# Output stores issued by ScalarE, and attention slots one group later, in a linear-attention block on eight cores

## The reference

```python
xn = layernorm(x)                      # no weight or bias here
q, k, v = xn @ Wq + bq, xn @ Wk + bk, xn @ Wv + bv
qf, kf = elu(q) + 1, elu(k) + 1        # heads of 128, chunks of 128 tokens
kv_ex, ksum_ex = sums of kf^T v and of kf over the chunks before
out = (qf kv_ex + causal(qf kf^T) v) / (qf ksum_ex + rowsum(causal(qf kf^T)) + 1e-6)
s = out @ Wo + bo
Wt = clip(round(W / mean|W|), -1, 1)   # ternary weights
g = silu((xn * ln_w + ln_b) @ Wt)
y = x + s * g
```

## Time and profile before

| | us |
|---|---|
| median of 3 runs | 2493.84 (2489.82 to 2498.37) |
| the profiled execution | 2509.68 |
| its span on the slowest core (core 4) | 2508.1 |
| spans of cores 0 to 7 | 2477.6, 2494.0, 2464.4, 2476.5, 2508.1, 2486.8, 2467.7, 2455.6 |
| mean granted TensorE clock, cores 0 to 7 | 0.990, 0.986, 0.990, 0.988, 0.985, 0.988, 0.991, 0.990 |

### The profile page before, as it was taken

The page is one execution under the profiler, slowest core; times in us unless marked ns, Lnnn a source line. Parts: engine busy times, 40 slices in busy tenths (PEclk is TensorE's granted clock), DMA queues, the critical chain, the costliest instruction groups (busy, mean ns, idle before and its releaser), DMA issues.

```text
span 2508.1 us, 38029 instructions; the slowest of 8 cores (2455.6 to 2508.1 us)
## 1 busy us (share of the span) xinstructions
PE 2397.4 (96%) x12618; PEld 1144.3 (46%) x12618; DVE 1168.0 (47%) x2448; ACT 698.8 (28%) x1241; POOL 245.1 (10%) x452
## 2 busy tenths in 40 slices
PE   5998999999999999998999999999999999999998
PEld 3444444444444444543444444554444445554443
DVE  6134766555521454554552144555554135554443
ACT  4144545223300343421220133441221024442000
POOL 1100000011111000011120000001111100000110
PEclk9999999999999999999999999999999999999999
DMA  8997877897755655569985554557998555555652
GB/s 213 209 208 173 171 174 169 187 214 201 177 102 88 97 91 96 102 160 213 212 173 106 94 93 91 113 104 182 228 183 164 91 105 99 101 103 113 161 158 73
DMA packets 264477, 363.31 MB, mean 145 GB/s; under 512 B 184416, under 2 KB 184416, under 8 KB 256096
## 3 DMA queue, kind: packets, MB, share of 16 engines
q0 software_dynamic: 56320, 201.36, 40.6%
q1 hardware_dynamic: 188672, 125.87, 22.8%
q10 hardware_dynamic: 19296, 33.66, 5.4%
HBM read 411.14 MB, written 41.94 MB: 181 GB/s over the span
## 4 chain that ended last, share of the span: by engine, by line
PE 73%; DMA 20%; DVE 4%; issue 2%; SPq 1%; ACT 0%; DVEq 0%; ACTq 0%; POOL 0%; POOLq 0%
PE pj L949 40%; PE pj L963 28%; DMA ktok<-kh 7%; DMA y<-xy 6%; DMA xy<-x 4%; DMA wscf<-wpr 2%; DVE bst L682 1%; PE px L991 1%; PE pa L977 1%; DMA ring<-w_v 1%; PE po L1010 1%; PE po L1007 1%; DVE to L853 1%; DVE to L858 1%; SPq L367 0%
## 5 line engine op out<-in xcount | busy, mean ns | idle before, releaser
L949 PE MATMUL pj<-ring,big 128*128 128x512 bf16 x6144 | 1351.0, 382 | 36.7 <-DVE to L853 27.2
L949 PEld LDWEIGHTS pj<-ring,big 128*128 128x128 bf16 x6144 | 601.8, 98 | 768.6 <-issue 65.8
L963 PE MATMUL pj<-big,ring 128*128 128x512 bf16 x4096 | 935.8, 383 | 0.0
L963 PEld LDWEIGHTS pj<-big,ring 128*128 128x128 bf16 x4096 | 394.1, 99 | 439.4 <-issue 18.9
L714 DVE TENSOR_TENSOR big<-pj,brow 128x512 bf16<-128x512 f32 x128 | 88.4, 691 | 329.3 <-PE pj L949 329.3
L839 DVE SCALAR_TENSOR_TENSOR tf<-pj,r,c_b 128x512 f32<-128x512 f32 x128 | 94.9, 747 | 175.4 <-PE pj L949 140.5
L533 ACT ACTIVATE ee<-pj,bk 128x512 f32<-128x512 f32 x128 | 88.0, 688 | 261.6 <-PE pj L963 261.6
L533 ACT ACTIVATE ee<-pj,bq 128x512 f32<-128x512 f32 x128 | 88.1, 688 | 259.1 <-PE pj L963 256.3
L564 ACT ACTIVATE sg<-tf 128x512 bf16<-128x512 f32 x128 | 79.2, 630 | 290.1 <-DVE tf L839 262.9
L464 POOL DMA_DIRECT2D ring<-w_qk x128 | 67.8, 544 | 930.4 <-PE pj L963 560.3
L861 DVE TENSOR_TENSOR xy<-to,xy 128x512 f32<-128x512 f32 x128 | 88.6, 692 | 121.6 <-DMA xy<-x 102.6
(11 more groups left out here) (79 smaller groups left out, 1442.0 us busy)
## 6 DMA issues: line engine op xcount, KB each, us to landing
ring<-w_qk POOLq DMA_DIRECT2D x128, 512.0 KB, 10.8
ring<-w_v POOLq DMA_DIRECT2D x64, 512.0 KB, 12.5
stg<-w_f SPq DMA_DIRECT2D x32, 1024.0 KB, 8.3
ring<-wscf POOLq DMA_DIRECT2D x64, 512.0 KB, 7.6
ring<-w_o POOLq DMA_DIRECT2D x64, 512.0 KB, 10.1
xy<-x ACTq DMA_DIRECT2D x128, 256.0 KB, 5.2
y<-xy POOLq DMA_DIRECT2D x128, 256.0 KB, 7.6
xln<-x SPq DMA_DIRECT2D x28, 1024.0 KB, 8.7
```

Source lines behind the costliest of these rows:

```text
L949: last = tensor.matmul(bank[:, :], src(k, m), ring[c % 3][:, k * 512:(k + 1) * 512], start=(k == 0), stop=(k == NT - 1))
L963: last = tensor.matmul(bank[:, :], ring[c % 3][:, base + k * 256:base + k * 256 + 128], x[:, k * T + tok:k * T + tok + 512], start=(k == 0 ...
```

## The change

`store_y` moves from POOL's program to ScalarE's. ScalarE calls it at the start of a step, for the output step before, so it waits there for that product (s_yd); the final waits for all stores move with it. `slot_units` counts slots from t - 1, so every `outputs`, `scores` and `outer`, with what VectorE, ScalarE and SyncE do for them, falls one slot later; LAST_SLOT becomes 69. `transpose_k` keeps its slots, 4h+2 and 4h+3. `outputs`, `scores` and `transpose_out` are now in odd slots, `outer` in even ones.

```diff
--- before.py
+++ after.py
@@ -30,7 +30,7 @@
 QK0 = 32
 FO0 = 96
 NCHUNK = 20
-LAST_SLOT = 68
+LAST_SLOT = 69
 NB = 3
 
 
@@ -115,7 +115,7 @@
 
 def slot_units(t):
 
-    hh, r = divmod(t, 4)
+    hh, r = divmod(t - 1, 4)
 
     def head(h, s):
         return (h, s) if 0 <= h < H else None
@@ -465,15 +465,6 @@
                                      in_=src[:, j * D:(j + 1) * D]
                                      ).then_inc(s_w[sl][j], 16)
 
-            def store_y(k):
-                pn, m = divmod(k, 8)
-                p, n = divmod(pn, 4)
-                g = p * MT + m
-                gpsimd.wait_ge(s_yd, k + 1)
-                gpsimd.dma_start(
-                    out=y_out[g * 128:(g + 1) * 128, n * 512:(n + 1) * 512],
-                    in_=xy[k % 4][:, :]).then_inc(s_ys[k % 4], 16)
-
             load_chunk(0)
             gpsimd.wait_ge(s_xn, 5)
             load_chunk(1)
@@ -484,14 +475,6 @@
                     c = p * NCHUNK + (i + 1) // 8 + 2
                     if i % 8 == 7 and c < NP * NCHUNK:
                         load_chunk(c)
-                    k = p * NG + i - 1
-                    if k > FO0 and (k % NG == NG - 1 or i - 1 >= FO0):
-                        n, m, o = of_fo(k % NG)
-                        if o:
-                            store_y((k // NG * 4 + n) * 8 + m)
-            store_y(NP * 32 - 1)
-            for i in range(4):
-                gpsimd.wait_ge(s_ys[i], 16 * (NP * 32 // 4))
 
         @block.scalar
         def _(scalar):
@@ -608,6 +591,15 @@
                                in_=x_in[g * 128:(g + 1) * 128, n * 512:(n + 1) * 512]
                                ).then_inc(s_xr[k % 4], 16)
 
+            def store_y(k):
+                pn, m = divmod(k, 8)
+                p, n = divmod(pn, 4)
+                g = p * MT + m
+                scalar.wait_ge(s_yd, k + 1)
+                scalar.dma_start(
+                    out=y_out[g * 128:(g + 1) * 128, n * 512:(n + 1) * 512],
+                    in_=xy[k % 4][:, :]).then_inc(s_ys[k % 4], 16)
+
             def copy_x(m):
 
                 p = m // MT
@@ -640,6 +632,12 @@
             for p in range(NP):
                 for i in range(NG):
                     t = i - QK0
+
+                    k = p * NG + i - 1
+                    if k > FO0 and (k % NG == NG - 1 or i - 1 >= FO0):
+                        n, m, o = of_fo(k % NG)
+                        if o:
+                            store_y((k // NG * 4 + n) * 8 + m)
                     if QK0 <= i < FO0:
                         evict_qk(p, t)
                     if 0 <= t <= LAST_SLOT:
@@ -659,6 +657,9 @@
                             load_xr(p, n, m)
                         if o and 2 <= m < 6:
                             load_xr(p, n, m + 2)
+            store_y(NP * 32 - 1)
+            for i in range(4):
+                scalar.wait_ge(s_ys[i], 16 * (NP * 32 // 4))
 
         @block.vector
         def _(vector):
```

## The result

Beside the kernel before on the same chip, the changed kernel takes 0.9942 of its time, with a 95% interval of 0.9914 to 0.9971. Of the 2493.84 us this is some 14 us less (2493.84 × 0.9942 = 2479). The medians of 19 runs each, 2489.34 and 2497.42 us, lie a little nearer to each other because some runs of both were disturbed (a whole die at a lower clock); the ratio leaves those out. The profiled execution took 2468.98 us, some 10 us less than the ratio gives. The forecast was 2440 us with a range of 2415 to 2478 us: right in sign, four times too large in size, and the time is outside the range.

What follows compares the result with a forecast made beforehand. The prediction took TensorE's waits on the slowest core, some 110 us idle, as the bound. From the profiled execution, 2509.7 − 43 (attention shift) − 27 (y stores) = 2440 us, range 2415 to 2478 us.

Steps and rivals of the forecast that it cites:

- What bounds the kernel: Slowest core: the matmul engine is busy 96% of the span, so the gain lies in TensorE's waits, some 110 us idle.
- What the shift gives: TensorE's ktok waits: 3.0 us more slack each removes 33.3 us, and 10 us of clock come back; −43 us.
- Together 7.3 us: What remains of the five ktok waits on TensorE that exceed the 3.0 us of slack gained.
- What the shift costs in pass 0: VectorE's state update behind ternary work in odd slots: still 0.6 us early, 0 us; 12 us if that cover is gone.
- The sign named for it: In pass 0, TensorE waits at L1007 for L550 or L759 would show the forecast wrong.
- I take 5 us: Time of a y store on ScalarE's queue, by the xy loads of equal size there; bounds 2.3 and 16.4 us.
- Rival (a): Moving the y stores gives nothing, as the DMA engines are shared and 0.89 busy: 2467 us, chance 0.13.
- The new wait is hardly longer than the old one: ScalarE's wait for s_yd: the product of m−1 comes only 3.45 us after that of m−2, whose store loads await anyway.
- Rival (c): On ScalarE's queue each refill stands behind a store, both taking 14.6 us: slower, 2547 us, chance 0.07.
- The term of −27 us: Gain from y stores on ScalarE's queue: 17 us at L853, 3.2 at L839, 3.4 at L1056, 3.4 of slow groups.
- the forecast's own marks: Among them: VectorE's 102.6 us at L861 below 50; stores about 5 us; ktok waits under 12 us; none at L1007.
- The other waits at L853 go: TensorE's output-projection eviction waits of 3.1 us and less vanish; of 27.2 us there, 17 go.

Runs made afterwards that it cites:

- `x_on_tensor`: Attention shift, y stores on POOL, TensorE transposing the normalised x in all passes in place of DMA transposes, against the kernel before: 0.9868 [0.9842, 0.9894].
- `wait_only`: Attention shift, y stores on POOL, ScalarE still made to wait for each product (s_yd), against the kernel before: 0.9864 [0.9836, 0.9892].

## Why the prediction was wrong, point by point

**What bounds the kernel: right.** From run to run the mean span went with TensorE's idle time: 106.8 us idle and 2507.2 with the loads one step later, 68.3 and 2456.2 after, 61.7 and 2449.9 with the shift, 39.3 and 2421.7 with the shift and copies. Only where TensorE got more work, in `x_on_tensor`, did it not.

**What the shift gives: right in mechanism, too large in size.** "Together 7.3 us" of ktok waits should stay; 5.2 us stayed on the slowest core and 2.0 us on average. The term was −43 us; the shift alone gave −24 us by its ratio (2493.84 × 0.0096; the interval is −13 to −34) and −28.9 us in the mean span of the two profiles (−26.7 over the runs of its ratio). Core 4 was chosen because it was slowest, and it was slowest because it had the most of these waits: with its 28.4 us for core 4's 40.6, of which 2.0 stay, the mean core has 26 us of waits to give and 7 of clock (10 × 28.4 / 40.6), 33 us. The time is that of whichever core is slowest in a run, and after the shift that is a core with other waits.

**What the shift costs in pass 0: the 0 us were wrong, and so was the reason.** It costs 3.3 to 3.5 us per core. The tight place that I worked out, with 0.6 us of cover under the ternary weights, held; TensorE waits at L1007 in slots before those begin. The step looked only at VectorE and the slots, and not at ScalarE's wait for its weights. The sign named for it, a wait at L1007 for L550, is there.

**"I take 5 us" for a store: wrong.** It was 8.5 and 8.4 us at m = 0 and 1, where it had been 11.5 and 9.1. Of the refill cycle 2.1 us went at m = 0, not 6. Here the rule of the Trainium skill that the prediction weighed ("DMA: Bandwidth & Descriptors", "Issuing engines are not separate DMA queues") was nearer: over all cores and places the median store stayed at 7.0 us, on either queue (the mean went from 8.0 to 7.1). Rival (a) has the same sum, and its 2467 us would have been the better forecast. Even (a) priced the move at nothing, though, and it cost time.

**"The new wait is hardly longer than the old one": true, and beside the point.** `wait_only` shows that the wait costs next to nothing. This is the step that failed. What the sentence left out is the opposite order: the store stands behind the *refill's* wait, which lasts as long as the store before it, and behind the LayerNorm's. Rival (c) had stores and refills in one line, but as transfers that each take 14.6 us, 29 us from product to refilled buffer; it is 17.0 to 18.7 us. What came late was the issue of the last refills, for m = 6 and 7, and the bill came at L839. The term of −27 us was in truth +11 us in the pair without transposes, some +6 us of mean span after the shift, and +12 us (2490.7 less 2478.8) alone; by the ratio, so on the slowest core, +27 us alone. With it, the forecast's own marks failed: VectorE waits 107.8 us, not under 50, and stores of over 10 us are there.

**"The other waits at L853 go": wrong in the main.** Moving the store takes 2.7 us from the cycle of m=0 (19.7 after the shift, 17.0), and the waits fall from 26.8 us after the shift to 18.0, of which 9.1 are the three stalls. So a part of the gain was there, and the stalls took it back. The rest needs the DMA transposes of x: 23.1 of the 26.8 us go with copies in their place.

**The sum** of the three profiles, −29 for the shift (with pass 0) and +6 for the stores, is −23 us, 2478.8 to 2456.2, but only because it is made of the same three numbers. A sum of its own comes from the two halves, each over the runs of its ratio and on one chip: mean spans of 2475.7 us before, 2449.0 with the shift and 2487.2 with the stores give −27 + 12 = −15 us. From the median, 2493.8 − 15 = 2479 us, as measured; that it fits so well is partly luck, as these are terms of the mean core and the time is the slowest one's. The forecast had also begun at the profiled execution, 15.8 us above that median. On the slowest core the halves do not add up as well (−24 and +27, beside −14; the intervals are ±10, ±12 and ±7 us): it stood 15 us over the mean core before, 17 with the shift and 29 with the stores alone. The stores bring the rare stalls, and the slowest of eight cores is often the one that has one.

**What stays open:** why a transpose of x of some 15 us takes 30 to 50 us now and then. It happens with stores on ScalarE's queue and with a chunk held back; that both move transfers onto the transposes is my reading, and which of them it takes was not settled. Twice the number of xy buffers, which would take the stores' time off the path altogether, was not tried.

## What to carry to other kernels

A DMA moved to another engine's queue moves into that engine's program: list what waits *ahead* of it there, not only what it makes wait, and follow the delay to the last buffer of the block and to the work behind it. Price the transfer itself as nearly unchanged: the mean store went from 8.0 to 7.1 us. And make the sum on the mean of the cores beside the slowest one: the slowest has more of the very thing that one is about to remove.

## What the runs showed of the hardware

- A DMA transpose of x between two SBUF tiles (0.5 MB, 17.1 us at the median in the shift alone) slows the transfers beside it more than a copy of the same size (12.8 us) does: with copies the refill cycle of m = 0 fell from 19.7 to 17.1 us and TensorE's waits for `evict_o` from 26.8 to 3.7 us. It took over 30 us now and then, 51.4 at the longest; no copy took over 28.6.
- The median time of a 256 KB store was the same issued on GpSimd's and on ScalarE's queue, 7.0 us. The first store of a block took 12.1 us behind a 2 MB ring chunk and 2.8 us with the chunk held back. An x load for the first two products of a block took 12 to 13 us on POOL's queue where ScalarE's took 7.0 to 7.5.
- The load of weights (1 MB) beside a ring chunk of 2 MB took 14 to 21 us, 20 us later 5 to 9 us; SyncE's queue was held 6.50 us by one transpose of k in that time.
